# A graph network on one core: the one-hots of the attention passes take their constants from PSUM

## What is computed

```python
q = (x @ Wq + bq).reshape(n, H, C)
k = (x @ Wk + bk).reshape(n, H, C)
v = (x @ Wv + bv).reshape(n, H, C)
e = (eattr @ We).reshape(-1, H, C)
kj = k[src] + e
alpha = jnp.sum(q[dst] * kj, axis=-1) / jnp.sqrt(jnp.float32(C))
m = jax.ops.segment_max(alpha, dst, num_segments=n)
a = jnp.exp(alpha - m[dst])
s = jax.ops.segment_sum(a, dst, num_segments=n)
a = a / (s[dst] + 1e-16)
vj = v[src] + e
out = jax.ops.segment_sum(a[..., None] * vj, dst, num_segments=n)
```

## Time and profile before

| | |
|---|---|
| device time, median of 3 runs | 6891.56 us |
| lowest and highest run | 6888.16, 6897.02 us |
| span of the profiled execution | 6876.3 us |
| PE busy | 4426.6 us (64%) |
| DVE busy | 4372.2 us (64%) |
| ACT busy | 1118.8 us (16%) |
| POOL busy | 4782.2 us (70%) |

### The profile page before, as it was taken

How to read it: one execution, slowest core, us unless ns; L and a number is a source line. 1 busy time by engine, 2 the same in 40 slices (tenths; PEclk the granted TensorE clock), 3 DMA queues, 4 the chain that set the end, 5 groups by cost and what they waited for, 6 DMA issues and landing times. The chain is left out here.

```text
span 6876.3 us, 149746 instructions
## 1 busy us (share of the span) xinstructions
PE 4426.6 (64%) x36620; PEld 3477.8 (51%) x36620; DVE 4372.2 (64%) x15731; ACT 1118.8 (16%) x4722; POOL 4782.2 (70%) x5116
## 2 busy tenths in 40 slices
PE   7996666666666667666666666667666666666665
PEld 5775444444444446444444444446444444444444
DVE  5556666666666666666666666666666666666666
ACT  3222111111111112111111111112111111111111
POOL 1224777777777775777777777775777777777776
PEclk8996555555555555555555555555555555555555
DMA  4553333333333333333333333333333333333333
GB/s 127 159 159 94 96 93 95 94 95 95 94 93 96 95 96 97 95 95 94 95 95 95 94 96 92 95 94 97 96 94 94 95 93 95 96 93 94 94 94 80
DMA packets 687682, 675.79 MB, mean 98 GB/s; under 512 B 369234, under 2 KB 506388, under 8 KB 687636
## 3 DMA queue, kind: packets, MB, share of 16 engines
q0 software_dynamic: 161600, 320.52, 19.1%
q1 hardware_dynamic: 496944, 301.76, 16.6%
q10 hardware_dynamic: 29092, 52.97, 2.6%
HBM read 652.96 MB, written 21.67 MB: 98 GB/s over the span
## 5 line engine op out<-in xcount | busy, mean ns | idle before, releaser
L1618 POOL DMA_INDIRECT Gall<-KV,sdn x4848 | 4645.5, 958 | 1518.0 <-issue 1368.8
L751 DVE TENSOR_TENSOR kj<-Gall,pE 128x512 f32<-128x512 f32 x603 | 414.7, 688 | 2022.8 <-DMA Gall<-KV,sdn 2020.8
L960 PE MATMUL pG<-O,vals 128*66 128x42 f32 (+1 forms) x10736 | 1292.3, 308 | 0.7 <-ACTq L1239 0.7
L960 PEld LDWEIGHTS pG<-O,vals 128*66 128x66 f32 (+1 forms) x10736 | 1201.0, 223 | 47.2 <-ACT vals L999 27.3
L945 PE MATMUL pY<-fw,Ob 128*42 128x6 bf16 (+1 forms) x4800 | 255.3, 176 | 1188.9 <-DVE cr L804 1188.9
L991 ACT ACTIVATE vals<-dd 128x16 f32<-128x16 f32 (+1 forms) x606 | 131.7, 217 | 4734.9 <-DVE dd L831 4726.3
L945 PEld LDWEIGHTS pY<-fw,Ob 128*42 128x42 bf16 x4800 | 220.8, 121 | 1243.1 <-issue 1243.0
L893 PE MATMUL pE<-bd,ea 128*128 128x256 f32 x1212 | 740.0, 714 | 13.6 <-PEq L1239 13.6
L898 PE MATMUL pE<-bd,ea 128*128 128x256 f32 x1212 | 642.7, 634 | 0.0
L952 PEld LDWEIGHTS pM<-Mb,OTs 42*128 42x128 bf16 x4800 | 176.3, 101 | 920.4 <-issue 920.4
L952 PE MATMUL pM<-Mb,OTs 42*128 42x6 bf16 (+1 forms) x4800 | 210.1, 163 | 513.4 <-DVE df L822 510.2
(11 more groups left out here) (221 smaller groups left out, 6428.2 us busy)
## 6 DMA issues: line engine op xcount, KB each, us to landing
db<-D SPq DMA_DIRECT2D x606, 256.0 KB
ea<-in_ea SPq DMA_DIRECT2D x606, 128.0 KB
Gall<-KV,sdn POOLq DMA_INDIRECT x4848
db<-D ACTq DMA_DIRECT2D x202, 256.0 KB, 3.7
qw<-QT SPq DMA_DIRECT2D x1818, 5.2 KB
dr<-in_dr SPq DMA_DIRECT2D x1212, 4.0 KB
ea<-in_ea SPq DMA_DIRECT2D x202, 64.0 KB, 3.6
sdn<-in_sdn SPq DMA_DIRECT2D x606, 12.0 KB
```

What stands on the lines that cost most here:

```text
L751: return e.tensor_tensor(kj[:, :, :], G[u][:, :, 0:64], pE[u][:, :].rearrange("p (j c) -> p j c", c=64), ALU.add)
L960: return e.matmul(out[0:AR, 0:W], vals[u][:, j, 0:AR], O[u][:, j, :], start=j == 0, stop=j == T - 1)
L1618: e.indirect_dma_start(G[u][:, j, :], None, kvtab, bass.IndirectOffsetOnAxis(ap=sdn[u][:, j:j + 1], axis=0)).then_inc(s_g[u], 16)
```

## The change

In the attention passes both one-hots read their constants from PSUM. The numbers 0 to 41 are copied once, in the setup, into columns 48 to 89 of the bank `pM` (`pIo`), and the table of bases per partition is written into the 399 columns behind them (`pBp`) where it was written into `bfp`. `O` stays the same instruction with its third operand in PSUM. `OTs` turns from a comparison with a scalar per partition (`tensor_scalar`) into a comparison of two tensors (`tensor_tensor`), the second being one PSUM column broadcast along 1024 elements. The mean pass keeps `iof` and `bfp` in SBUF and the scalar form. No instruction changes its place; one is added, in the setup of DVE. The hand-written drain keeps its `O` with `iof` (once per layer).

```diff
-        assert self.idle + W <= self.nc and self.smax <= 512
+        assert self.idle + W <= self.nc and 6 * T + W + self.smax <= 512
...
     pMe = pM[:, 0:6 * T]
+    pIo = pM[:, 6 * T:6 * T + W]
+    pBp = pM[:, 6 * T + W:6 * T + W + SM]
...
         e.tensor_copy(dnarrow, dwide).then_inc(su_V, 1)
+        e.tensor_copy(pIo, iof[:, 0:W]).then_inc(su_V, 1)
...
+        columns = pIo if att else iof[:, 0:W]
...
             return e.scalar_tensor_tensor(
                 O[u][:, :, :], sdn[u][:, T:2 * T].unsqueeze(2).to_broadcast([128, T, W]),
                 bf[:, bass.ds(s.value(), 1)],
-                iof[:, 0:W].unsqueeze(1).to_broadcast([128, T, W]), ALU.subtract, ALU.is_equal)
+                columns.unsqueeze(1).to_broadcast([128, T, W]), ALU.subtract, ALU.is_equal)
...
             if att:
                 ge16(e, s_l, NL, s)
-            else:
-                ge16(e, s_d, 1, s)
+                return e.tensor_tensor(OTs[u][:, :, :].rearrange("p j m -> p (j m)"), db[u][:, :],
+                                       pBp[:, bass.ds(s.value(), 1)].to_broadcast([128, T * 128]), ALU.is_equal)
+            ge16(e, s_d, 1, s)
             return e.tensor_scalar(OTs[u][:, :, :].rearrange("p j m -> p (j m)"), db[u][:, :],
                                    bfp[:, bass.ds(s.value(), 1)], None, ALU.is_equal)
...
-        e.tensor_scalar(bfp[:, :], bf[:, :], pmf[:, 0:1], None, ALU.add).then_inc(bfp_V, 1)
+        e.tensor_scalar(pBp, bf[:, :], pmf[:, 0:1], None, ALU.add).then_inc(bfp_V, 1)
```

More of the change, by code:

```diff
@@ L194, in build @@
                  "base", "base1", "over", "base2", "tbase", "tblock", "n0", "n1", "n2", "ntr", "me0", "onb",
-                 "cb", "cbh0", "cbh1", "rowf", "rowf4", "row1", "row2", "row12", "rowin", "thirds", "below", "third", "rowbase", "narrow"] + [f"qz{u}" for u in range(3)]
+                 "cb", "cbh0", "cbh1", "rowf", "rowf4", "row1", "row2", "row12", "rowin", "thirds", "below", "third", "rowbase", "narrow", "iop"] + [f"qz{u}" for u in range(3)]
                 + [f"flg{u}" for u in range(3)] + [f"one{u}" for u in range(3)])
```

## The result

| | before | after |
|---|---|---|
| device time, median | 6889.86 us (4 runs, 6886.35 to 6897.02) | 6814.85 us (4 runs, 6813.86 to 6815.26) |
| span of the profiled execution | 6876.3 us | 6813.4 us |
| gathers, busy | 4645.5 us | 4579.8 us |
| DVE busy | 4372.2 us | 4794.8 us |

The changed kernel is faster: ratio 0.9893, 95% interval 0.9879 to 0.9907. The direction and the mechanism were right, the time was not. (The 6889.86 us are the median of one execution more than stood in the table ahead of the prediction, which had 6891.56.)

What follows compares the result with a forecast made beforehand. POOL's indirect gathers were taken to set the pace. Terms of -55.8, -12.3, +4.4, +0.4, +0.3 and +4.2 sum to -58.8 us, taking the span to 6817.5 and, with 15.3 us carried over, the time to 6832.8 us (range 6818 to 6852).

Steps and rivals of the forecast that it cites:

- The step that failed: From span to device time: the runs' median lies 15.3 us above the profiled span, carried over to reach 6832.8 us.
- lower bound of 6820: The forecast's own fast bound, 6820 us: every gather at the median length and no holds by flg.
- stalls behind O: Attention passes: 129 gathers held until 1.37 us after O starts; with iof in PSUM taken as gone, -55.8 us.
- stalls behind OT: Attention passes: 118 gathers stretched beside the fast OT; as tensor_tensor it loses its hold on POOL, -12.3 us.
- POOL's stop at a layer's start: Block 3's node numbers wait for block 0's O, behind two longer OTs: 1.5 us for each of three layers, +4.4.
- flg: A short DVE operation that holds gathers starting just after it; at the later phase 78 hits, 5.5 us, +4.2 net.
- node phases' operations beside gathers: Node-phase operations beside the first gathers of a layer; the forecast's sum has no change for them.
- drain, setup and the rest: End of a layer, the last kj waiting on one late OT, +0.4 us; setup copy and PSUM output, +0.3 us.
- rival 1: O goes on holding gathers, at a later phase: 475 stalls instead of 124, +92.8 us, total 6977 us; 5 in 100.
- The second: The new OT itself holds gathers, every block by some 0.6 us, 362 us in all: about 7190 us; 2 in 100.
- Rival 3: Half the gain: excess only partly O's hold, or small two-SBUF operations enter the window, +24 us: 6857 us; 6 in 100.
- Rival 4: Nothing to measure: an unseen wait, PE and DVE on one PSUM bank, takes as much: 6892 us; 4 in 100.

Runs made afterwards that it cites:

- the second trace: The kernel before, run again unchanged with its trace: median 6887.25 us (10 runs); the profiled execution took 6885.18 us with a span of 6883.3.
- O alone: The changed kernel with the old fast scalar OT and its column in SBUF, so only O reads PSUM: 6819.77 us, ratio 0.9896 to the kernel before.
- the OT half alone: The changed kernel with O reading iof in SBUF again, so only OT is the new PSUM comparison: 6889.1 us, ratio 0.9997 to the kernel before.
- the column in SBUF: The changed kernel with the new OT reading its broadcast column from bfp in SBUF, not PSUM: 7126.99 us, ratio 1.0343 to the kernel before.
- the same kernel: The changed kernel with node numbers in their own tile, loaded after the gathers of block s-3: 6802.42 us, ratio 0.9867; in slow jobs 1.0554 to 1.0565.

## Why the prediction was wrong, and what of it was right

**The step that failed** is the last one of the sum: "The median of the runs lies 15.3 us above the profiled span, and I carry that over." I took the difference for something that lies around the span and that the change leaves alone, and every run shows 1.8 to 1.9 us there. The other 13.4 us were the luck of the execution that I had read: it was about as fast as the fastest of 29, and at least part of that was fewer stalls (68.1 us of them behind O and OT, 79.4 in the second trace), which is just what the change takes away. The changed kernel has none behind O and OT, and its runs lie within 1.4 us of each other where the before's lie within 10.7. The medians fell by 75.0 us, the profiled spans by 62.9. With 1.9 us around it, my own span of 6817.5 gives 6819.4 us, 4.6 above the measured median: of the 18.0 us that the forecast was off, 13.4 are this step and 4.6 the terms. The forecast's lower bound of 6820 does not follow from its words either: every gather at the median and no flg is -69 + 5.1 us, which gives 6828, or 6814 with 1.9 us around the span.

**The terms**, by my counts of both traces:

| term | forecast | measured |
|---|---|---|
| stalls behind O | -55.8 | -55.8 (129 to 0) |
| stalls behind OT | -12.3 | -12.3 (118 to 0) |
| POOL's stop at a layer's start | +4.4 | +3.6 (13.3 to 16.9 us over three) |
| flg | +4.2 | +1.9 (22 stalls, 1.3 us; 46, 3.2 us) |
| node phases' operations beside gathers | 0 | +0.5 (1.7 to 2.2) |
| drain, setup and the rest | +0.7 | -0.8 (the first gather starts 0.6 earlier, the end follows the last gather 0.3 sooner) |
| span | -58.8 | -62.9 |

More than half of the 4.1 us by which the span was missed is flg, counted at 78 stalls and met 46 times. It is the same count as in rival 1, with every kj left where it stood against the gathers. The start of a layer was near in sum and not in its parts (-0.1, +2.5 and +1.2 us where 1.5 was expected three times); against O alone, which has the short OT and stops for 12.2 us, the new OT costs 4.7 us.

**What would show it.** Mean of a gather 944 to 946: 945. Longest about 1.1: 1.21. OT 1.22, O 0.55: as said. Wait ahead of kj 0.6 to 0.8 us shorter per block: 485.3 / 603 = 0.80. POOL's gap near 6.2 where it was 4.7: that one, the second layer's, is 7.17. Long gathers only beside flg and node phases: so.

**The rivals.** The first fell with O alone, where O keeps its form and its scalar and holds nothing; its price, O's hold at the later phase, is what the OT half alone measures, 76 and not 147 us of stalls. The second fell with the 1060 gathers beside the new OT. Its price is what the column in SBUF measures: 7127 where I had 7190, mostly since one gather of a block waits 0.53 us, not 0.6. Rival 3, holds by other operations in the new phase, was flg and the node phases alone (the terms above): no other gather takes over 0.96 us. Rival 4, a hidden wait between DVE's constants and PE in one bank of PSUM, would have shown in O, OT or PE. O is no longer, and OT's 1214 ns are those of a tensor_tensor in SBUF (1219 with the column in SBUF). PE is busy 70.3 us more in the changed kernel, but 89.0 more with OT's column in SBUF, and 0.3 more in O alone, which reads the same bank: so that goes with the later DVE step and not with the bank.

## What to carry to other kernels

Before you carry the gap between a median and a profiled span over to a forecast, ask what it is made of: here time minus span was 1.9 us in each run, and in the rest was the very stall that the change removes, seen on an execution that had few of them. If a kernel's runs spread by ten and more microseconds with the same instructions, a stall that depends on the phase of two engines is worth looking for; the gain on the median can then be larger, or smaller, than on the one execution that was profiled. A count of such stalls at a new phase needs the phase to be known: here an operation that waits for a DMA moved as well, and the count gave nearly double. And where POOL's indirect gathers set the pace, ask of every operation of DVE whether it has two tensors in SBUF. O's second operand alone, which costs DVE nothing, brought 71 of the 75 us and lost nothing in the jobs of the other kind; the new OT, 2.5 times as long, added 5 us (6819.77 to 6814.85, in two jobs, the intervals of the ratios overlap) and lost up to 1.2% there.

## What the runs showed of the hardware

- A tensor_tensor with both inputs in SBUF, even with one of them a single broadcast column, holds an indirect gather until it ends: one that takes 0.94 us took up to 2.0, and all 600 held ones end 0.81 to 0.83 us after it. The same with the column in PSUM holds none of 1060 gathers that overlap it. The operation's own length is alike, 1219 and 1214 ns.
- A tensor_scalar in its fast form (1024 elements in 0.48 us) also holds a gather that started 0.39 to 0.48 us before it (63 of 75), where an operation with two tensors in SBUF holds none (0 of 49, 0 of 54).
- The kernel's 6890 us are not the only answer of the machine: for a stretch of time four jobs on four chips took 9100 to 9180 us, with engines standing for up to 13.6 us at waits that the profile leaves without a releaser, gathers no longer than before, and a mean pass without gathers that took no longer. A ratio measured in one kind of job says little on the other: -1.3% and +5.5% for the same kernel.
